# Third attention's scan: one of a quad's two weighings moved from VectorE to ScalarE and GpSimd

## The reference, cut to what matters

```
def rosa_scan(x):
    """y[r,c] = x[r,c] * (y[r-1,c-1] + 1) on the lower triangle of each [T,T] matrix"""
...
def rosa_attn_score(x, tau):          # tau = 0.1
    x = x + p                          # p[r, c] = c / (r + 1)
    x = jnp.where(mask, -jnp.inf, x)   # above the diagonal
    return jax.nn.softmax(x / tau, axis=-1)
```

## Time and profile before

| | |
|---|---|
| time, median of 3 runs | 4862.11 us (4853.09 to 4879.02) |
| profiled execution: its time, its span | 4898.38 us, 4896.7 us |
| busy over the span: PE, PEld, DVE, ACT, POOL | 3668.0, 2319.2, 3133.7, 1855.0, 1135.0 us |
| second-block quads of the two groups | 3016 to 3490 us and 3914 to 4388 us |
| weighings (L1844) | 768 of about 686 ns, 256 of them of second blocks |

### The profile page before, as it was taken

One profiled execution on the slowest core, in us unless ns is written; L12 is line 12 of the kernel. 1 busy time (PEld: TensorE's weight loads), 2 busy tenths in 40 slices (PEclk: granted clock), 3 DMA queues, 4 the chain that ended last, 5 costly groups with the idle time before them and its releaser, 6 DMA issues. The chain is left out here.

```text
span 4896.7 us, 134252 instructions
## 1 busy us (share of the span) xinstructions
PE 3668.0 (75%) x55119; PEld 2319.2 (47%) x55119; DVE 3133.7 (64%) x7733; ACT 1855.0 (38%) x4296; POOL 1135.0 (23%) x1987
## 2 busy tenths in 40 slices
PE   5999999951366663077745799999879999993398
PEld 1222222210244443044432577887547788773366
DVE  7777777747522234233356789999778999983633
ACT  1655555541122210022222566555346655541000
POOL 1000000000000006533310465333235543320000
PEclk6999999975567765599965899999869999995599
DMA  5222222000000011111121000000000000001000
GB/s 119 41 45 44 46 46 45 9 6 0 0 0 0 0 52 43 39 48 47 47 74 47 8 13 8 13 8 6 5 6 11 11 9 8 8 6 41 0 0 34
DMA packets 89291, 121.86 MB, mean 25 GB/s; under 512 B 16020, under 2 KB 59929, under 8 KB 88432
## 3 DMA queue, kind: packets, MB, share of 16 engines
q1 hardware_dynamic: 75632, 90.65, 7.8%
q0 software_dynamic: 13088, 23.06, 1.6%
HBM read 69.65 MB, written 45.04 MB: 23 GB/s over the span
## 5 line engine op out<-in xcount | busy, mean ns | idle before, releaser
L1920 ACT ACTIVATE s_E<-s_Y,s_M 128x9 f32<-128x9 f32 (+38 forms) x2048 | 656.6, 392 | 625.0 <-DVE s_M L1833 623.2
L343 DVE TENSOR_REDUCE half_max<-bm 128x1 f32<-128x512 f32 x1024 | 653.5, 685 | 232.1 <-PE bm L264 227.7
L1734 PE MATMUL g_x<-s_ik,s_iqm 128*32 128x1 f32 (+63 forms) x16384 | 677.3, 280 | 30.7 <-DVE g_o L1816 11.6
L455 ACT ACTIVATE E<-sc 128x1024 f32<-128x1024 f32 x512 | 521.0, 1024 | 362.9 <-PE sc L278 352.4
L1828 DVE SCALAR_TENSOR_TENSOR s_Y<-s_Y,g_x 128x9 f32<-128x9 f32 (+38 forms) x2048 | 578.5, 282 | 47.9 <-DVE s_Y L1828 1.5
L1746 PE MATMUL g_p<-mats,s_E 128*128 128x128 f32 x3072 | 448.9, 283 | 38.0 <-ACT s_E L1920 33.1
L264 PE MATMUL bm<-ks,qs 96*128 96x512 bf16 x1024 | 416.9, 410 | 75.4 <-DVE half_max L343 44.5
L1734 PEld LDWEIGHTS g_x<-s_ik,s_iqm 128*32 128x32 f32 x16384 | 395.1, 116 | 158.1 <-issue 83.2
L1746 PEld LDWEIGHTS g_p<-mats,s_E 128*128 128x128 f32 x3072 | 339.3, 144 | 103.8 <-ACT s_E L1920 58.0
L264 PEld LDWEIGHTS bm<-ks,qs 96*128 96x128 bf16 x1024 | 99.3, 97 | 553.1 <-DVE half_max L343 458.8
L1833 DVE TENSOR_REDUCE s_M<-s_Y 128x4 f32<-128x8 f32 (+56 forms) x512 | 351.1, 686 | 0.3 <-DVE s_Y L1828 0.2
(11 more groups left out here) (355 smaller groups left out, 5639.6 us busy)
## 6 DMA issues: line engine op xcount, KB each, us to landing
d_parts<-parts SPq DMA_DIRECT2D x8, 1536.0 KB, 5.9
qs<-d_parts SPq DMA_DIRECT2D x96, 128.0 KB, 7.9
ks<-d_parts SPq DMA_DIRECT2D x96, 128.0 KB, 11.5
me_xg<-d_xs SPq DMA_DIRECT2D x144, 65.0 KB
mc_yb<-d_ys SPq DMA_DIRECT2D x8, 1024.0 KB
resid<-in_x SPq DMA_DIRECT2D x8, 512.0 KB, 7.9
rden<-d_den POOLq DMA_DIRECT2D x16, 256.0 KB, 4.0
m_w_gu<-in_gate_up SPq DMA_DIRECT2D x1, 4096.0 KB, 12.6
```

The lines of the kernel that those rows point to most:

```text
L343: dve.tensor_reduce(half_max[n // SETS % 2][:, idx // 2, idx % 2:idx % 2 + 1], bm[n % 2][:, :], AX_X, ALU.max).then_inc(max_done, 1)
L455: act.activation(E[:, G % 2, h, :], sc[n % 2][:, :], ACT.Exp, scale=0.25).then_inc(exp_done, 1)
L1734: mm = pe.matmul(x_ps[u % 3][32 * b:32 * (b + 1), rho % 2, 0:n + 1], iqm[n // WINDOW % 2][:, b, x0:x0 + D, :], s.ik[:, b, rho, 0:n + 1], s ...
L1920: act.activation(E[:, m % 2, rho, 0:m + 1], Y[:, D * (m % YR) + rho, 1:2 + m], ACT.Exp, bias=M[:, D - 1 + D * m + rho:D + D * m + rho]).th ...
```

## The change

The second block of a quad is no longer weighed by VectorE. ScalarE copies it from PSUM into `prob` (`take_late`), and GpSimd multiplies it there in place (`weigh_late`). New semaphores `copied` and `late_done` count these; `p_done` counts first blocks alone. TensorE's second turn waits for the copy of the quad before, and `values` waits for both counts.

```diff
+        def late(m):
+            return max(0, m - P)
...
@@ tensor: turn(m, jt)
                     if jt == 0:
                         pe.wait_ge(exp_done, D * (m + 1))
-                    if i >= 2:
-                        pe.wait_ge(p_done, i - 1)
+                        if m >= 2:
+                            pe.wait_ge(p_done, m if late(m) else m - 1)
+                    elif late(m):
+                        pe.wait_ge(copied, late(m))
+                    else:
+                        pe.wait_ge(p_done, m)
...
@@ tensor: values(c, g)
-                        pe.wait_ge(p_done, turns((c + 1) * CHUNK))
+                        pe.wait_ge(p_done, (c + 1) * CHUNK)
+                        if late((c + 1) * CHUNK):
+                            pe.wait_ge(late_done, late((c + 1) * CHUNK))
...
@@ vector: slot n
                     if 0 <= n - 2 < QUADS:
-                        weigh(n - 2, 0)
+                        weigh(n - 2)
                     if n < QUADS:
                         recur(n, 2)
-                    if 0 <= n - 2 < QUADS and blocks(n - 2) == 2:
-                        weigh(n - 2, 1)
-                    if n < QUADS:
                         recur(n, 3)
...
@@ scalar
+                def take_late(m):
+                    c = m // CHUNK
+                    act.wait_ge(turned, turns(m) + 2)
+                    if m % CHUNK == 0 and c >= 2:
+                        act.wait_ge(av_done, CHUNK * (c - 1))
+                    act.activation(prob[c % 2][:, m % CHUNK, 1, :, :, :, :].rearrange("p r b i h -> p (r b i h)"),
+                                   p_ps[(turns(m) + 1) % 2][:, :, :].rearrange("p r l -> p (r l)"), ACT.Copy).then_inc(copied, 1)
...
@@ scalar: slot n, ahead of exps(n - 1)
+                    if 0 <= n - 2 < QUADS and blocks(n - 2) == 2:
+                        take_late(n - 2)
...
@@ gpsimd
+                def weigh_late(m):
+                    c = m // CHUNK
+                    pool.wait_ge(copied, late(m) + 1)
+                    if m % CHUNK == 0:
+                        pool.wait_ge(w_done, W_EXPS * (c + 1))
+                    pr = prob[c % 2][:, m % CHUNK, 1, :, :, :, :].rearrange("p r b i h -> p (r b i) h")
+                    pool.tensor_tensor(pr, pr, W[c % 2][:, 1, m % CHUNK, :, :].rearrange("p r l -> p (r l)").unsqueeze(2)
+                                       .to_broadcast([P, D * NB * D, HEADS]), ALU.mult).then_inc(late_done, 1)
...
@@ gpsimd: slot n, first in the slot
+                    if 0 <= n - 2 < QUADS and blocks(n - 2) == 2:
+                        weigh_late(n - 2)
```

More of the change, by code:

```diff
@@ L1676, in scan_rows @@
         arg_done, w_done = sem("arg_done"), sem("w_done")
+        copied, late_done = sem("copied"), sem("late_done")
         f_full, f_free, least_done, less, f_exp, split, summed, half, rec, carried, added = (
@@ L1834, in maximum, with weigh @@
                                       AX_X, ALU.max, negate=True).then_inc(max_done, 1)
-                def weigh(m, jt):
-                    i = turns(m) + jt
+                def weigh(m):
+                    i = turns(m)
                     c = m // CHUNK
                     dve.wait_ge(turned, i + 1)
-                    if m % CHUNK == 0 and jt == 0:
+                    if m % CHUNK == 0:
                         dve.wait_ge(w_done, W_EXPS * (c + 1))
@@ L1843, in weigh @@
                             dve.wait_ge(av_done, CHUNK * (c - 1))
-                    dve.tensor_tensor(prob[c % 2][:, m % CHUNK, jt, :, :, :, :].rearrange("p r b i h -> p (r b i) h"),
+                    dve.tensor_tensor(prob[c % 2][:, m % CHUNK, 0, :, :, :, :].rearrange("p r b i h -> p (r b i) h"),
                                       p_ps[i % 2][:, :, :].rearrange("p r (l h) -> p (r l) h", h=HEADS),
-                                      W[c % 2][:, jt, m % CHUNK, :, :].rearrange("p r l -> p (r l)").unsqueeze(2).to_broadcast(
+                                      W[c % 2][:, 0, m % CHUNK, :, :].rearrange("p r l -> p (r l)").unsqueeze(2).to_broadcast(
                                           [P, D * NB * D, HEADS]), ALU.mult).then_inc(p_done, 1)
@@ L1907, in weights @@
                     if c >= 2:
-                        act.wait_ge(p_done, turns((c - 1) * CHUNK))
+                        act.wait_ge(p_done, (c - 1) * CHUNK)
+                        if late((c - 1) * CHUNK):
+                            act.wait_ge(late_done, late((c - 1) * CHUNK))
                     for jt in range(2):
```

## The result

The changed kernel takes 4896.21 us in the median (4892.06 to 4896.94, 5 runs), where the kernel before took 4862.11: 1.0062 of before, 95% interval 1.0041 to 1.0084. It is slower, by about 30 us (the ratio follows the means of the runs; the medians are 34 us apart). In a later session, in which before lay at 4889.63 us, it was 4916.39 us: 1.0056 (1.0040 to 1.0073), 27 us. I forecast 4866 us and no change that can be told, with a range up to 4892.

A forecast was written before the change was run, and what follows sets the result against it. TensorE was taken to bound the kernel from quad 138 on, VectorE only quads 128 to 137. Two groups x (0 for early quads + 1 for late GpSimd + 1 at group's end) = +4 us: 4862 + 4 = 4866 us, range 4847 to 4892.

The forecast's parts named there:

- TensorE sets the pace from quad 138 on, and VectorE's relief is worth next to nothing: Quads 138 to 255: TensorE runs at its own pace; a faster VectorE could fill only about 2 of 444 us a group.
- The saving of VectorE: Each quad with a second block: dropping its weighing saves VectorE 0.37 us, 95 us in all, nearly all beside TensorE.
- The 70 us that I named as a sign: Long stretch: VectorE's busy time falls by about 118 x 0.6 = 70 us, its waits for TensorE growing by as much.
- The loop: Turn, copy, exponentials, next turn: 3.06 us at 152 columns, 3.32 at 229; hidden behind TensorE by 0.21 and 0.44 us.
- Quads 128 to 137: Ten early quads: bound moves from VectorE to a 3.0 us loop; 0 us, between -2 and +2 per group.
- The multiplication: GpSimd's new work on 128x512 elements: 1.29 us each, making its work 308 of 444 us in the long stretch.
- The only one who waits for a multiplication is `values` of the next chunk.: GpSimd's queue: only TensorE's `values` at the next chunk waits for a multiplication, with 1.8 us of room.
- The rest: Where four slots with `arguments` come before, GpSimd is still behind: 1 us a group.
- the group's end: Last quads of a group, no scores between turn and values: 3.1 us instead of the weighing's 1.8; +1 us a group.
- The copy at 1.08 us: Slower rival: ScalarE's copy costs what a strided one does, making the loop 0.48 us longer; 47 us, 4909 us; chance 0.08.
- the bound by its load: Slower rival: GpSimd's multiplication costs 2.6 us and sets the pace of early quads; 28 us, 4894 us; chance 0.05.
- VectorE as the bound: Faster rival: VectorE sets the pace, so its relief is worth up to 95 us, 4767 us; chance 0.07.

The follow-up runs named there:

- small_second_weighing: The kernel before, with VectorE's second weighing cut to an eighth of its elements and no other engine loaded; 0.9993 of before (0.9978 to 1.0008).
- gather_first: The changed kernel with GpSimd's second gather of a chunk moved ahead of that slot's multiplication; 1.0013 of before (1.0000 to 1.0025).
- copy_twice: `gather_first` with ScalarE's copy made twice, the second waiting for the first; 1.0124 of before (1.0099 to 1.0148), 54 us over `gather_first`.

## Why the prediction was wrong, step by step

- **TensorE sets the pace from quad 138 on, and VectorE's relief is worth next to nothing.** Right, and shown: `small_second_weighing` gives 1.9 us a group. I said at most 2 us in the long stretch and what the ten early quads give.
- **The saving of VectorE.** 0.37 us a quad was right: 118 x 0.37 = 44 us, and `gather_first`, in which quad 128 is 3.3 us earlier than before, has VectorE at 373.4 instead of 419.55 us in the long stretch, 46 less. The 70 us that I named as a sign took 0.6 us a quad and forgot that the dependent recurrences count as busy.
- **The loop.** Right to 0.05 us, and closer than I had a right to expect. `copy_twice` shows room of 0.20 us near quad 145 and 0.47 near quad 225, where I had 0.21 at 152 columns and 0.44 at 229.
- **Quads 128 to 137.** I counted 0 between -2 and +2 us; +2.2 came, of which 1.6 went with the gather's move, and 0.65 stayed. So the loop itself was within the bounds. My 3.0 us a slot for before was a little short: from turn to turn the ten take 31.24 us, 3.12 each.
- **The multiplication.** 1.09 us instead of 1.29: the slope of the earlier trace rows, 2.16 ns an element, is too steep for it; from 0.64 us for 256 elements to 1.09 for 512 it is 1.76. The row of 1024 elements, which gave 1.06, was the better one. Nearest in form was a row that I did not use: GpSimd's `mask` (L1968), a multiplication of 152 elements with both inputs broadcast, takes 446 ns, where the addition of 128 full elements takes 457. The line through 256 and 512 elements gives 0.46 us for 152. The error was 0.2 us on the safe side, and is not why the time came out longer.
- **The step that failed: "The only one who waits for a multiplication is `values` of the next chunk."** I followed the multiplication's result and not its place in the queue. GpSimd takes its queue in order, and behind the multiplication in the slot of the second gather stand the two additions whose sum TensorE's `quotient` wants in that same slot. The chain is 5.17 us long against TensorE's 4.2 to 4.9. With my price of 1.29 us it would have come to some 5.4 us, so the trace of before had all that it takes to see it. It costs 0.9 us a chunk near quad 156 and 0.35 near quad 244, with one chunk of 2 us (quad 148) and one of 1.3 (quad 180), where `arguments` come before. With quad 132 the quotient's slots are 12.6 us of the 13.4 that the first group lost, and moving the gather took back 10.8 of them. In my sum this term was missing. The wait that I did price, `values` at a chunk's start, does not occur in the changed kernel: from quad 144 on the first slot of each chunk is within 0.02 us of before. (ScalarE's `weights` waits for multiplications too, those of the chunk two before; no trace has a wait for them.)
- **The rest**, 2.6 us a group with the gather moved, is quads 128 to 137 (0.65), quads 144 to 159 (1.7) and 0.3 in quads 176 to 191. In the first group the 1.7 are 1.0 at quad 148, the quotient behind late `arguments`, and 0.7 at quad 152, where `values` starts 0.1 us behind the end of a multiplication. I had 1 us for this. For the group's end I had 1 us too: from the turn of quad 255 to the end of the scan's last `add` on GpSimd the changed kernel's four groups take 0.3 to 2.0 us more than those of before, but so do the groups of `small_second_weighing` (0.2 and 0.9 more), which has nothing new there, so this term is not shown.
- **The rivals.** The copy at 1.08 us did not come. GpSimd did not become the bound by its load (276 of 444 us), but one wait on it did, on the slower side, which neither rival named. VectorE as the bound is refuted by `small_second_weighing`. My range ended at 4892, 30 us above the median, and I called this half of the slower rivals' loss; half of 47 and 32 us is 24 and 16. The rule of the Trainium skill ("Perfetto Trace Analysis", "Identifying the Most-Contended Engine") to relieve the engine of the highest occupancy, with weight loads (and MFU, which I did not work out) counted for TensorE, would have relieved VectorE. The runs do not agree: in `small_second_weighing` VectorE fell from 94% to 83% (367.66 of 444 us) and the time stayed at 0.9993.

## What to carry to other kernels

An instruction that waits, put at the head of a queue that is worked off in order, delays what stands behind it by the wait and its own length. List what stands behind it in every kind of slot and who needs each of these when, not only who needs its own result. Two engines that look full are told apart by who waits for whom, and a kernel with seven eighths of the suspected work left out settles it. Where a slot's length stops growing with the data, as the 5.17 us did, it is a chain of fixed pieces, and its terms can be read off one slot.

## What the runs showed of the hardware

GpSimd's queue is worked off in order: it stood idle for 2.23 us ahead of a multiplication that waited for its copy, with the gather behind it ready to run, and with the gather first the quotient's slot fell from 5.17 to 4.30 us.

GpSimd's multiplication in place, with a broadcast second input, took 0.64 us for 256 elements and 1.09 for 512, where its addition of 256 elements with both inputs full took 0.73 us. No run here tells whether the operation or the broadcast makes the difference.

The same kernel before had medians of 4862.11, 4894.4 and 4889.63 us in three sessions, 0.7% apart, while the slots without a quotient, from quad 138 on, are within 0.05 us of before in both traces of the changed kernel, but for one of 1.1 us. What differs between sessions must for the most part lie elsewhere. The first turn of the scan stands at 2721.6 us in the trace of before and at 2692.5 and 2709.5 in the two of the changed kernel, behind the same code, and the first 128 quads of a group, which the change leaves alone, take 291.6 to 294.2 us in these three traces. No run here shows why.
